# The attention stage of a five-engine kernel written out for all 32 images, without its loop over four images

## The reference

```
x = x + _L0_conv_ref(_gn(x), ...)   # a 3x3 convolution with weights mixed per image
x = x + _L1_conv_ref(_gn(x), ...)   # a 3x3 convolution with quantised weights and partial sums
x = x + _L2_conv_ref(_gn(x))        # a two-dimensional DCT
x = x + _L3_conv_ref(_gn(x), ...)   # attention, 4 heads of 16, over 784 tokens
```

```
xs = xn.reshape(B, C, H * W).transpose(0, 2, 1)
qkv = (xs @ w_proj.T + b_proj).reshape(B, H * W, N_HEADS, 3 * D_K)
q, k, v = jnp.split(qkv, 3, axis=-1)
attn = jnp.einsum('bihk,bjhk->bijh', q, k) * D_K ** 0.5
attn = jax.nn.softmax(attn, axis=2)
h = jnp.einsum('bjhk,bijh->bihk', v, attn)
h = h.reshape(B, H * W, N_HEADS * D_K)
h = h @ w_out.T + b_out
h = h * jax.nn.sigmoid(h)
h = h + xs
```

## Time and profile before

| | us |
|---|---|
| median of 3 executions | 1787.89 |
| lowest and highest | 1787.02, 1790.91 |
| the profiled execution | 1786.88 |
| its span, first to last instruction | 1785.0 |
| PE busy | 1603.3 |
| DVE busy | 1295.2 |
| ACT busy | 1021.8 |
| POOL busy | 455.0 |
| attention, first scores matmul of image 0 | at 631.70 |
| first scores matmul of image 4, where the loop begins | at 771.03 |
| first scores matmul of image 28, behind the loop | at 1644.62 |

### The profile page before, as it was taken

The page is one execution under the profiler, slowest core; times in us unless marked ns, Lnnn a source line. Parts: engine busy times, 40 slices in busy tenths (PEclk is TensorE's granted clock), DMA queues, the critical chain, the costliest instruction groups (busy, mean ns, idle before and its releaser), DMA issues.

```text
span 1785.0 us, 35090 instructions
## 1 busy us (share of the span) xinstructions
PE 1603.3 (90%) x10848; PEld 732.7 (41%) x10848; DVE 1295.2 (73%) x2666; ACT 1021.8 (57%) x1401; POOL 455.0 (25%) x364
## 2 busy tenths in 40 slices
PE   0699879999686799999999999999999999999997
PEld 0333335555675144444434444443443444444332
DVE  5677557787787677777777767776777777777772
ACT  0100156765232057777767767776776776777776
POOL 0400011110300403324233332342332423334212
PEclk9999989999897589999999999999999999999998
DMA  8111166664000433223422333223332243223300
GB/s 202 35 49 52 31 104 104 104 107 79 1 0 1 63 41 54 37 44 47 62 45 34 51 48 54 44 34 54 49 50 45 35 62 52 39 44 48 61 12 19
DMA packets 71264, 93.40 MB, mean 52 GB/s; under 512 B 23516, under 2 KB 64340, under 8 KB 70960
## 3 DMA queue, kind: packets, MB, share of 16 engines
q1 hardware_dynamic: 67728, 89.59, 30.6%
q0 software_dynamic: 3360, 1.61, 1.3%
HBM read 9.00 MB, written 6.42 MB: 9 GB/s over the span
## 4 chain that ended last, share of the span: by engine, by line
PE 76%; DVE 8%; ACT 4%; DMA 4%; issue 4%; SPq 3%; POOL 0%; DVEq 0%; ACTq 0%; POOLq 0%
PE ps L1056 19%; PE ps L1046 17%; PE ps L991 15%; PE ps L866 8%; PE ps L890 4%; PE ps L905 3%; DVE arena L1436 2%; PE ps L1012 2%; SPq L437 2%; DMA arena<-arena 2%; PE ps L952 2%; DMA x<-x_in 2%; ACT arena L684 2%; PE ps L1029 1%; PE ps L1020 1%
## 5 line engine op out<-in xcount | busy, mean ns | idle before, releaser
L1436 DVE TENSOR_REDUCE arena<-ps 128x1 f32<-128x392 f32 x1600 | 825.9, 561 | 272.4 <-PE ps L991 261.2
L797 ACT ACTIVATE arena<-ps 112x784 f32<-112x784 f32 x896 | 704.3, 822 | 260.6 <-PE ps L1046 254.8
L991 PE MATMUL ps<-arena 112*128 112x392 bf16 x1536 | 485.8, 343 | 15.5 <-DVE arena L1436 7.9
L1046 PE MATMUL ps<-arena 114*112 114x392 bf16 x1792 | 445.5, 335 | 20.2 <-issue 14.4
L1056 PE MATMUL ps<-arena 112*32 112x392 f32 x3584 | 391.9, 509 | 0.5 <-ACT arena L797 0.5
L991 PEld LDWEIGHTS ps<-arena 112*128 112x128 bf16 x1536 | 149.4, 97 | 368.4 <-DVE arena L1436 301.7
L1046 PEld LDWEIGHTS ps<-arena 114*112 114x112 bf16 x1792 | 225.1, 133 | 123.3 <-ACT arena L797 43.1
L890 PE MATMUL ps<-arena 96*128 96x392 f16 x768 | 142.2, 336 | 22.7 <-DMA arena<-arena 17.1
L684 ACT ACTIVATE arena<-ps,magic,arena 128x784 f32<-128x784 f32 x128 | 128.1, 1004 | 38.5 <-PE ps L890 38.0
L866 PE MATMUL ps<-arena 128*64 128x392 f32 (+1 forms) x768 | 139.5, 505 | 3.9 <-DMA arena<-arena 3.9
L1056 PEld LDWEIGHTS ps<-arena 112*32 112x32 f32 x3584 | 70.7, 108 | 142.5 <-issue 140.7
(11 more groups left out here) (142 smaller groups left out, 1346.7 us busy)
## 6 DMA issues: line engine op xcount, KB each, us to landing
arena<-arena SPq DMA_DIRECT2D x504, 73.5 KB, 2.7
arena<-arena SPq DMA_DIRECT2D x256, 84.2 KB, 2.8
x<-x_in SPq DMA_DIRECT2D x8, 784.0 KB, 22.3
out<-x SPq DMA_DIRECT2D x16, 392.0 KB, 3.0
arena<-arena SPq DMA_DIRECT2D x252, 24.5 KB, 2.4
arena<-arena SPq DMA_DIRECT2D x256, 1.5 KB
arena<-arena SPq DMA_DIRECT2D x16, 225.0 KB, 3.4
arena<-arena SPq DMA_DIRECT2D x16, 224.8 KB, 2.9
```

The costliest lines, as they stand in the source:

```text
L797: nc.scalar.activation(probs[w % 2][:, 2 * pair:2 * pair + 2, :], two(2 * place, rows=slice(0, TT)), ACT.Exp).then_inc(s_taken, 1)
L991: last = nc.tensor.matmul(ps[:, bank, 0:CH], q[0:ROWS_L, h, it * 128:(it + 1) * 128], k[0:ROWS_L, h, c * CH:(c + 1) * CH], start=True, sto ...
L1046: last = nc.tensor.matmul(ps[0:TT, 2 * place + j, 0:CH], ks[s % 4][0:ROWS_ALL, h, jt * TT:(jt + 1) * TT], qs[s % 4][0:ROWS_ALL, h, c * CH: ...
L1436: nc.vector.tensor_reduce(mx[img % 2][:, c, v:v + 1], scores, AX.X, ALU.max).then_inc(s_mf, 1)
```

## The change

`l3_steps` calls the step function of each engine for `s` from 0 to 31 with `i` as `None`, so every awaited count and every address of the attention stage is a constant. The loop, its bounds `STEP_LOOP` and DVE's `LINKS3` go; DVE uses the same `l3_steps` as the others. The order of the operations on each engine, the buffers and the other stages' loops stay.

```diff
--- before.py
+++ after.py
@@ -363,17 +363,11 @@
 
             return 9 * n_qk(s) - 8 + 2 * n_out(s)
 
-        STEP_LOOP = 4, B // 4 - 2, 4
         PAIR_LOOP = 4, NP // 2 - 3, 2
 
-        def l3_steps(step, eng):
-
-            for s in range(4):
-                step(s, None)
-            with eng.Fori(0, STEP_LOOP[1]) as i:
-                for j in range(4):
-                    step(4 + j, i)
-            for s in range(B - 4, B):
+        def l3_steps(step):
+
+            for s in range(B):
                 step(s, None)
 
         def pair_steps(step, eng):
@@ -496,7 +490,7 @@
                     sp.dma_start(out_dram[:, bass.ds(pr, 1), :].rearrange("c n t -> c (n t)"),
                                  xp(pr)).then_inc(s_out, 16)
 
-            l3_steps(l3_dma, sp)
+            l3_steps(l3_dma)
             sp.wait_ge(s_done, NP)
             sp.dma_start(out_dram[:, NP - 1, :], x[:, NP - 1, :]).then_inc(s_out, 16)
             sp.wait_ge(s_out, 16 * NP)
@@ -635,7 +629,7 @@
                 wait_apart(pool, s_pool, n(2))
                 nc.gpsimd.tensor_tensor(xp(p), xp(p), gate[:, :], ALU.add).then_inc(s_done, 1)
 
-            l3_steps(l3_pool, pool)
+            l3_steps(l3_pool)
 
 
         @block.scalar
@@ -801,7 +795,7 @@
                         if what == U_ACC0:
                             take_heads(s, 0, lin(lambda t: NW * t + NT, s, i, 4))
 
-            l3_steps(l3, act)
+            l3_steps(l3)
             take_heads(B - 1, 1, NW * B)
             act.wait_ge(s_done, NP - 1)
             n = at_ring(B - 1, NU - 1) + 1
@@ -1145,7 +1139,7 @@
                     else:
                         extra(after, second)
 
-            l3_steps(l3, pe)
+            l3_steps(l3)
             n = at_ring(B - 1, NU - 1) + 1
             pe.wait_ge(s_taken, n)
             weigh(B - 1, NW - 1)
@@ -1493,11 +1487,7 @@
                     if u == U_RECIP[s % 2] and s >= 1:
                         reciprocals(lin(lambda t: 16 * t, s, i, 4))
 
-            for s in range(4):
-                l3(s, None)
-            looped(l3, STEP_LOOP, LINKS3)
-            for s in range(B - 4, B):
-                l3(s, None)
+            l3_steps(l3)
 
 
             for c in range(2):
@@ -1513,8 +1503,6 @@
             v.tensor_tensor(xp(NP - 1), xp(NP - 1), gate[:, :], ALU.add).then_inc(s_done, 1)
 
 
-
-LINKS3 = 4 * 3
 
 
 def pack(a):
```

## The result

| | before | after |
|---|---|---|
| median us | 1789.40 of 4 executions | 1765.97 of 4 |
| lowest and highest | 1787.02, 1792.93 | 1762.61, 1769.09 |
| profiled execution | 1786.88 | 1766.60 |
| its span | 1785.0 | 1763.9 |
| images 4 to 27 (first scores matmul of 4 to that of 28) | 873.59 | 851.74 |

The ratio is 0.9867, with a 95% interval of 0.9841 to 0.9893: faster by 1.3%. The forecast was 1765.0 us, in a range from 1758 to 1771 us. The executions of this kernel differ by 6.5 us; what makes them differ is not shown.

What follows compares the result with a forecast made beforehand. The attention stage was taken as bound by PE's matmul stream, interrupted by the loop's jumps. Span 1785.0 - 22.9 = 1762.1 us, plus 1.88 us around it 1764.0, plus 1.0 us for the median: 1765.0 us, range 1758 to 1771 us.

Steps and rivals of the forecast that it cites:

- rival 1: Even images' wait for the denominators goes as well, as in image 2: 8.0 us more gain, 1757.0 us; chance 0.07.
- Which interrupts PE: Attention stage: PE's own matmul stream bounds it, the loop's jump interrupts it; five waits, 14.4 us in all.
- Rivals 3 and 4: Rival 3: code fetched in line is late, 1791.9 us, chance 0.04; rival 4: jump isn't the cause, 1787.9 us, 0.02.
- PE's loop written out, 22.9 us: Images 4 to 27 of the attention go from 873.59 to 850.68 us, 14.4 us of it idle time.
- the jumps of the others: Jumps of DVE, ACT, GpSimd and Sync: costed at nothing beyond the iterations' excess already counted.
- The cost of one jump: At each loop head PE idles 2.66 to 3.12 us while code is fetched again, plus slow clock and pipeline refill.
- Even images at 35.94 us: Written-out even images priced by image 28, against 36.23 us for image 6 in the loop: 0.29 us back each.
- Clock at 1.00 throughout: Expected sign in the changed kernel's profile: granted clock at 1.00 throughout the attention stage.
- rival 2: Loop's 0.85 us denominators wait stays or worse, or part of jump cost returns: 1768.5 or 1773.5 us; chance 0.14.

Runs made afterwards that it cites:

- the shift: Denominators' product behind unit 16 of even images instead of 14: on the kernel after 1756.63 us, on the kernel before (all loops) 1782.00 us.
- the kernel with three iterations: Kernel before, but the loop has three iterations over eight images on every engine, two jumps back: 1785.47 us; with the denominators' product two units later 1766.91 us.
- the kernel with the store moved: Kernel after, but Sync stores a finished output pair behind the copies of the next even step, so in an odd image: 1759.09 us.

## Why the prediction was right, and where its reasons were not

**Total and sign.** 1765.0 us was forecast and 1765.97 us measured; 23.4 us between the medians, 22.9 us by the sum. Images 4 to 27 went from 873.59 to 851.74 us, 850.68 us by the sum. The stated range was a little worse than the prediction says: rival 1's 1757.0 us lies outside it, and with that rival 0.20 is left out, not less. That the total came within 1 us was in part luck, as the items on the cost of a jump and on the even images show.

**Which interrupts PE.** Right: the pauses stood at the five jumps and are gone, and fetching code in a line stayed hidden (46 packets of q8, some 48 by the estimate, 16 to 23 us apart; no "issue" wait in front of any scores matmul that is worth a row). Rivals 3 and 4 did not come.

**PE's loop written out, 22.9 us.** The size was right, the owner incomplete. I costed the jumps of the others at nothing beyond PE's. That is about true while PE jumps: they add 1.9 us with the shift and 5.4 us without it. But the step reads as if PE's own code were the cause, and PE alone written out took 1785.54 us. PE's restart covers the others'. When PE does not jump, each of the others reaches it on its own way: PE feels 1.8 to 2.0 us of DVE's 3 us and 0.6 to 0.7 us of ACT's 2 us at each head, and the later start of GpSimd's DMAs in between, and these about add up. The gain needed DVE's, GpSimd's and Sync's loops gone as well as PE's; for ACT's it is not clear.

**The cost of one jump.** The prediction left 22.9 - 3.5 = 19.4 us for the jumps, 3.9 us each, and my first expectation had 2.93 + 1.21 us from the first jump. The parts were right: idle time and half a clock. As a price for a kernel it was 5.1 us in the medians of the shifted kernels, since the clock's part was not a constant.

**Even images at 35.94 us.** Right in the sum, wrong as a picture. I took one image for twelve. They came out between 35.33 and 36.04 us, and one at 39.93 us; image 28 itself, from which the price was read, went to 38.54 us though its code did not change. The average over images 4 to 26 is (851.74 - 12 x 34.94) / 12 = 36.04 us, which is why the sum held. The common even image was shorter than the 36.23 us of the loop by more than the 0.29 us forecast, and image 6 gave some 4 us of it back. With the shift before and after, the images 4 to 27 took 863.52 and 841.98 us: 21.5 us are the jumps, and of 21.85 us in all only 0.3 us is left for the waits. By the medians the jumps are 25.4 us of 23.4 us in all, and nothing is left. The prediction had 12 x 0.29 = 3.5 us there. So the jumps were priced too low and the waits too high, and the two errors nearly cancelled.

**Clock at 1.00 throughout.** Wrong. It fell behind the waits of 1.49 and 1.62 us. I named the wait as rival 1's gain and rival 2's loss, but not that a wait of this length can take the clock with it, which doubled its price in image 28 and tripled it in image 6.

## What to carry to other kernels

When all engines run the same loop, write it out on all of them or measure each: the pauses overlap, and removing the visible one alone brought 3 us of 23 here. Before a loop is written out, look for the gap at its iterations' heads and count code packets there; 3 to 6 us at a body of 145 us is 2 to 4%, but a jump within code just run cost nothing that showed here. And where a small DMA feeds the bound engine, ask which large store is issued within a microsecond of it: moving either one was worth another 7 to 9 us here, for a few lines or a single number.

## What the runs showed of the hardware

The granted clock could fall to half behind idle times of PE of about 1 us, but did not always: the shortest was 0.92 us, with PE alone written out, with another of 0.76 us in the two microseconds before it; waits of 1.00, 1.03 and 1.09 us were followed by it in the kernel with three iterations and others of 1.08 and 1.00 us there were not. Pauses of 2.92 and 3.00 us at a jump were followed by full clock with all loops and the shift, and others of 2.8 to 3.7 us by 3.4 or 6.8 us of half. The stretches at half clock in images 4 to 28 were 3.4 to 10.2 us long, and each cost about half its length.

The restart of an engine at a jump took about 3 us on PE (2.7 to 3.7 us) and on DVE (3.0 to 3.1 us), and left ACT idle for 1.9 to 2.0 us; between them, PE's covered the others'. A small DMA issued within a microsecond of a 392 KB store landed up to 4.8 us after its issue, and after 2.9 us at most in the kernel with the store moved. A wait that follows a jump may be put down in the profile to a semaphore that was long satisfied.
